# Router products on raw turned rows, softmax and the two largest in two parts, and an early indirect transfer

## The reference, cut to what matters

```python
x = x + graph_attention(ctx, layernorm(x), ...)          # layer 1: two GAT layers, 8 heads
x = x + expert_ffn(layernorm(x), w_router, w_gate, w_up, w_down)   # layer 2
# expert_ffn, for each of the 1024 tokens h = layernorm(x):
probs = softmax(h @ w_router)         # 8 experts
weights, experts = top_k(probs, 2)    # the two largest
# out = sum over the two experts of weight * scale * ((silu-gated gate) * up) @ down
x = x + similarity_attention(ctx, layernorm(x), Wq, Wk, gamma)     # layer 3
x = x + attention_and_experts(layernorm(x), ...)                   # layer 4
```

## Time and profile before

| | us |
|---|---|
| median of 3 runs | 1102.59 |
| lowest and highest | 1101.93, 1104.66 |
| the profiled execution | 1102.88 |
| its span | 1101.0 |
| TensorE busy in the span | 1006.5 (91%) |
| VectorE busy | 868.8 (79%) |
| ScalarE busy | 613.7 (56%) |
| GpSimd busy | 430.9 (39%) |

### The profile page before, as it was taken

One profiled execution on the slowest core, in us unless ns is written; L12 is line 12 of the kernel. 1 busy time (PEld: TensorE's weight loads), 2 busy tenths in 40 slices (PEclk: granted clock), 3 DMA queues, 4 the chain that ended last, 5 costly groups with the idle time before them and its releaser, 6 DMA issues.

```text
span 1101.0 us, 20158 instructions
## 1 busy us (share of the span) xinstructions
PE 1006.5 (91%) x5934; PEld 821.6 (75%) x5934; DVE 868.8 (79%) x2642; ACT 613.7 (56%) x1748; POOL 430.9 (39%) x372
## 2 busy tenths in 40 slices
PE   4788877999996489999999999999998999999997
PEld 2455545466663368999999999999887888888886
DVE  6999996577773889878777877777868888788877
ACT  4789983533232377777787777777952222222231
POOL 5798892633321233323332333222422232233231
PEclk9968887699998699999999999999999999999999
DMA  9700003011113111010101000000011111111111
GB/s 286 257 1 2 1 2 110 27 47 49 44 39 117 60 39 49 1 39 2 49 1 40 13 23 1 2 1 1 15 30 29 44 43 52 48 43 44 56 43 38
DMA packets 49459, 49.25 MB, mean 45 GB/s; under 512 B 4896, under 2 KB 42464, under 8 KB 49376
## 3 DMA queue, kind: packets, MB, share of 16 engines
q1 hardware_dynamic: 45888, 40.83, 11.8%
q0 software_dynamic: 2208, 6.03, 1.8%
q10 hardware_dynamic: 1280, 1.38, 0.5%
HBM read 43.11 MB, written 5.11 MB: 44 GB/s over the span
## 4 chain that ended last, share of the span: by engine, by line
PE 71%; DVE 12%; ACT 7%; POOL 5%; issue 4%; DMA 1%; SPq 0%; DVEq 0%; ACTq 0%; POOLq 0%
PE bank L57 13%; PE bank L58 13%; PE bank L59 13%; PE bank L957 6%; PE bank L978 4%; PE bank L852 4%; PE bank L860 4%; PE bank L879 4%; PE bank L967 3%; PE bank L979 2%; POOL rest L1418 2%; POOL alpha L1421 1%; DVE alpha L1626 1%; ACT alpha L1069 1%; ACT alpha L1054 1%
## 5 line engine op out<-in xcount | busy, mean ns | idle before, releaser
L1483 POOL TENSOR_TENSOR rot_s<-swap,rq 128x512 f32<-128x512 f32 x64 | 88.5, 1384 | 194.7 <-ACT swap L1261 194.6
L1137 ACT ACTIVATE silu<-bank 128x512 f32<-128x512 f32 x66 | 39.4, 598 | 173.6 <-PE bank L59 173.6
L2066 DVE TENSOR_TENSOR o_ring<-bank,o_ring 128x256 fp32r<-128x256 f32 x128 | 54.2, 424 | 80.2 <-ACT o_ring L1290 78.7
L1274 ACT ACTIVATE prob<-prob,pmin 128x128 f32<-128x128 f32 (+1 forms) x256 | 113.3, 447 | 5.4 <-DVE pmin L2047 5.4
L957 PE MATMUL bank<-kv,norm 128*128 128x128 f32 (+1 forms) x512 | 106.1, 330 | 6.1 <-DVE norm L2040 5.9
L1889 DVE SCALAR_TENSOR_TENSOR xs<-bank,wt,xs 128x256 f32<-128x256 f32 x264 | 109.0, 476 | 0.1
L1439 POOL TENSOR_TENSOR gate_r<-gate_w,gate_r 128x256 fp32r<-128x256 f32 x31 | 36.4, 1175 | 177.3 <-ACT gate_r L1130 177.3
L1290 ACT ACTIVATE o_ring<-bank 128x256 fp32r<-128x256 f32 x128 | 48.3, 378 | 76.4 <-PE bank L979 76.3
L57 PE MATMUL bank<-wo_r,o_ring 128*128 128x256 f32 x256 | 82.5, 322 | 0.0
L1867 DVE TENSOR_TENSOR hidf<-silu,bank 128x512 f32<-128x512 f32 x66 | 45.4, 688 | 44.9 <-ACT silu L1137 43.2
L2059 DVE TENSOR_SCALAR prob<-prob,pinv 128x128 f32<-128x128 f32 (+1 forms) x256 | 76.9, 343 | 4.6
(11 more groups left out here) (304 smaller groups left out, 3087.0 us busy)
## 6 DMA issues: line engine op xcount, KB each, us to landing
gate_w<-in_Wg SPq DMA_DIRECT2D x33, 128.0 KB, 2.1
up_w<-in_Wu SPq DMA_DIRECT2D x33, 128.0 KB, 2.3
down_w<-in_Wd SPq DMA_DIRECT2D x33, 128.0 KB, 2.3
w_all<-in_w_gate SPq DMA_DIRECT2D x8, 512.0 KB, 10.5
w_all<-in_w_up SPq DMA_DIRECT2D x8, 512.0 KB, 10.3
w_all<-in_w_down SPq DMA_DIRECT2D x8, 512.0 KB, 10.6
wq_g<-in_Wq SPq DMA_DIRECT2D x4, 1024.0 KB, 5.8
wo_g<-in_Wo SPq DMA_DIRECT2D x4, 1024.0 KB, 5.5
```

The lines of the kernel that those rows point to most:

```text
L1274: ins = act.activation(prob[:, u % 4, nt * P:nt * P + (nt + 1) * P], prob[:, u % 4, nt * P:nt * P + (nt + 1) * P], ACT.Exp, bias=pmin[:, u ...
L1483: pool.tensor_tensor(rot_s[:, m % 2].rearrange("p (b n) -> p b n", b=2), swap[:, m % 2].rearrange("p (b n) -> p b n", b=2), bcast(tab[:, 1 ...
```

## The change

There are four parts. First, `turn_graph` turns `xs` (raw rows) and not `norm`; the mean is taken out of the router's weights instead (`router_means` on TensorE and a subtraction on VectorE into `wr0`), and rstd is multiplied into the logits. Second, TURN_AT and ROUTE_AT of graphs 0 to 2 are other steps. Third, softmax and the two largest are done for the first six tiles (LEAD) and then for the last two, whose logits go to bank 3; `normalise_graph(B - 1)` goes behind the weights in `router0`, and five memsets go ahead of the last `add_x1`. Fourth, GpSimd sends one indirect transfer of a constant row to `xg` before its wait for the stores. SP's program is not changed.

```diff
-        NORM_AT, TURN_AT, ROUTE_AT = (ALL, ALL + 2, ALL + 10), (ALL + 2, ALL + 4, ALL + 11), (ALL + 4, ALL + 6, ALL + 12)
+        NORM_AT, TURN_AT, ROUTE_AT = (ALL, ALL + 2, ALL + 10), (ALL + 1, ALL + 3, ALL + 7), (ALL + 4, ALL + 6, ALL + 8)
+        LEAD = T - NT
                 def turn_graph(b):
-                    pe.wait_ge(S["norm_done"], NT * b + NT)
+                    pe.wait_ge(S["x1_added"], b + 1)
...
-                                              norm[:, NT * b + nt, c * P:c * P + P], ident[:])
+                                              xs[:, NT * b + nt, c * P:c * P + P], ident[:])
                     mm.then_inc(S["normT_ready"], NT)
+                def router_means():
+                    pe.wait_ge(S["const_in"], 16 * 5)
+                    pe.wait_ge(S["mean_set"], 1)
+                    pe.wait_ge(S["z_copied"], ALL)
+                    for c in range(HC):
+                        mm = pe.matmul(bank[2][:, T * E0:(T + 1) * E0], work[:, 0:P], wr0[:, c, :], start=c == 0, stop=c == HC - 1)
+                    mm.then_inc(S["wr_mean"], 1)
                 def route_graph(b):
                     pe.wait_ge(S["normT_copied"], NT * b + NT)
                     if b == 0:
-                        pe.wait_ge(S["const_in"], 16 * 5)
-                        pe.wait_ge(S["z_copied"], ALL)
+                        pe.wait_ge(S["wr_centred"], 1)
                     for t in range(NT * b, NT * b + NT):
+                        dst = bank[3][:, (t - LEAD) * E0:(t - LEAD + 1) * E0] if t >= LEAD else bank[2][:, t * E0:(t + 1) * E0]
...
+                    if b == B - 2:
+                        mm.then_inc(S["lead_ready"], 1)
...
+                    if k == ROUTE_AT[0] - 2:
+                        router_means()
 # ScalarE
+            act.wait_ge(S["lead_max"], 1)
+            act.activation(route[:, 0, 0:LEAD, 0:E0], route[:, 0, 0:LEAD, 0:E0], ACT.Exp).then_inc(S["lead_exp"], 1)
             act.wait_ge(S["rmax_done"], 1)
-            act.activation(route[:, 0, :, 0:E0], route[:, 0, :, 0:E0], ACT.Exp).then_inc(S["rexp_done"], 1)
+            act.activation(route[:, 0, LEAD:T, 0:E0], route[:, 0, LEAD:T, 0:E0], ACT.Exp).then_inc(S["rexp_done"], 1)
 # GpSimd
+            pool.memset(first_row[:], 0).then_inc(S["row_set"], 1)
+            pool.wait_ge(S["row_set"], 1)
+            pool.indirect_dma_start(
+                out=xg[:, 2, 0:P], out_offset=None, in_=ident_in,
+                in_offset=bass.IndirectOffsetOnAxis(ap=first_row[:], axis=0)).then_inc(S["xg_lead"], 16)
+            pool.wait_ge(S["xg_lead"], 16)
             pool.wait_ge(S["rows_out"], 16 * B)
 # VectorE, in the loop: normalise_graph(b) of graphs 0 to 2 goes ahead of elu(j)
+                    if k == ROUTE_AT[0] - 1:
+                        dve.wait_ge(S["wr_mean"], 1)
+                        dve.tensor_tensor(wr0[:], wr0[:], bcast(bank[2][:, T * E0:(T + 1) * E0], 1, HC), ALU.subtract
+                                          ).then_inc(S["wr_centred"], 1)
                     if (r := round_at(k, 20)) is not None:
+                        if r == 2 * B - 1:
+                            dve.wait_ge(S["g_elu"], QUADS * 2 * B)
+                            dve.memset(ones[:], 1.0)
+                            dve.memset(padded[:], -1.0)
+                            dve.memset(marks[:, :, T:], 0.0)
+                            chain.link(dve.memset(same_e[:], 1.0))
+                            dve.memset(same_e[:, :, 0:1], 0.0)
                         add_x1(r)
...
                 measure(2 * B - 1)
-                dve.memset(ones[:], 1.0)
...
-                normalise_graph(B - 1)
                 chain.restart()
+            def scaled_logits(ts, logits, ready, rms, done):
+                R = route[:, 0, ts, 0:E0]
+                dve.wait_ge(ready, 1)
+                dve.wait_ge(S["x_rms"], rms)
+                chain.link(dve.tensor_tensor(R, logits.rearrange("p (t e) -> p t e", e=E0), bcast(rstd[:, ts], 2, E0), ALU.mult))
+                chain.link(dve.tensor_reduce(rcol[:, 0, ts], R, X, ALU.max))
+                dve.tensor_tensor(R, R, bcast(rcol[:, 0, ts], 2, E0), ALU.subtract).then_inc(done, 1)
+            def two_largest(ts, ready):
+                R = route[:, 0, ts, 0:E0]
+                dve.wait_ge(ready, 1)
+                chain.link(dve.tensor_reduce(rcol[:, 1, ts], R, X, ALU.add))
+                chain.link(dve.reciprocal(rcol[:, 2, ts], rcol[:, 1, ts]))
+                chain.link(dve.tensor_tensor(padded[:, ts, 0:E0], R, bcast(rcol[:, 2, ts], 2, E0), ALU.mult))
+                for t in range(ts.start, ts.stop):
+                    dve.max(rtop[:, t, :], padded[:, t, 0:8])
...
+                for t in range(ts.start, ts.stop):
                     dve.match_replace(kept[:, t, :], rtop[:, t, :], padded[:, t, :], -2.0)
...
+                scaled_logits(slice(0, LEAD), bank[2][:, 0:LEAD * E0], S["lead_ready"], 2 * B - 1, S["lead_max"])
+                two_largest(slice(0, LEAD), S["lead_exp"])
+                scaled_logits(slice(LEAD, T), bank[3][:, 0:NT * E0], S["logit_ready"], 2 * B, S["rmax_done"])
+                two_largest(slice(LEAD, T), S["rexp_done"])
                 dve.tensor_tensor(chosen, kept[:, :, 0:E0], padded[:, :, 0:E0], ALU.not_equal).then_inc(S["chosen_done"], 1)
...
                 dve.scalar_tensor_tensor(weight, chosen, 0.25, padded[:, :, 0:E0], ALU.mult, ALU.mult)
+                normalise_graph(B - 1)
                 dve.wait_ge(S["count_ready"], 1)
 # VectorE, at the kernel's start
+            dve.memset(work[:, 0:P], 1.0 / D).then_inc(S["mean_set"], 1)
```

More of the change, by code:

```diff
@@ L127, in build @@
         eps = sb("eps", [P, 2])
+        first_row = sb("first_row", [P, 1], I32)
         minus_half = sb("minus_half", [P, NT])
@@ L1569, in finish_second, with normalise_graph @@
                 chain.link(dve.tensor_scalar(bT1[:], bT[:], -1.0, None, ALU.add))
+            def normalise_graph(b):
+                dve.wait_ge(S["x_rms"], B + b + 1)
+                for t in (NT * b, NT * b + 1):
+                    dve.tensor_scalar(norm[:, t, :], xs[:, t, :], mv[:, t, 0:1], rstd[:, t:t + 1],
+                                      ALU.subtract, ALU.mult).then_inc(S["norm_done"], 1)
             def graph_attention():
@@ L1667, in add_x1 @@
                     dve.tensor_tensor(rows, FEAT[:], rows, ALU.add).then_inc(S["x1_added"], 1)
[L1669 to L1674, removed]
                 measure(0)
@@ L1703, in graph_attention @@
                         divide(j)
+                    for b in range(B - 1):
+                        if k == NORM_AT[b]:
+                            normalise_graph(b)
                     if (j := quad_at(k, 4)) is not None:
                         elu(j)
+                    if k == ROUTE_AT[0] - 1:
+                        dve.wait_ge(S["wr_mean"], 1)
+                        dve.tensor_tensor(wr0[:], wr0[:], bcast(bank[2][:, T * E0:(T + 1) * E0], 1, HC), ALU.subtract
+                                          ).then_inc(S["wr_centred"], 1)
                     if (r := round_at(k, 20)) is not None:
+                        if r == 2 * B - 1:
[5 more added lines that the diff above has]
+                            dve.memset(same_e[:, :, 0:1], 0.0)
                         add_x1(r)
@@ L1720, in graph_attention @@
-                chain.restart()
-            def router0():
-                R = lambda j: route[:, j, :, 0:E0]
-                logits = bank[2][:, 0:T * E0].rearrange("p (t e) -> p t e", t=T)
-                dve.wait_ge(S["logit_ready"], 1)
-                chain.link(dve.tensor_reduce(rcol[:, 0, :], logits, X, ALU.max))
-                dve.tensor_tensor(R(0), logits, bcast(rcol[:, 0, :], 2, E0), ALU.subtract).then_inc(S["rmax_done"], 1)
-                dve.wait_ge(S["rexp_done"], 1)
-                chain.link(dve.tensor_reduce(rcol[:, 1, :], R(0), X, ALU.add))
-                chain.link(dve.reciprocal(rcol[:, 2, :], rcol[:, 1, :]))
-                chain.link(dve.tensor_tensor(padded[:, :, 0:E0], R(0), bcast(rcol[:, 2, :], 2, E0), ALU.mult))
-                for t in range(T):
+                chain.restart()
@@ L1737, in router0 @@
                 chain.link(dve.engine_nop())
-                chain.link(dve.memset(rtop[:, :, K0:8], -1.0))
-                for t in range(T):
+                chain.link(dve.memset(rtop[:, ts, K0:8], -1.0))
+                for t in range(ts.start, ts.stop):
                     dve.match_replace(kept[:, t, :], rtop[:, t, :], padded[:, t, :], -2.0)
                 chain.link(dve.engine_nop())
+            def router0():
+                scaled_logits(slice(0, LEAD), bank[2][:, 0:LEAD * E0], S["lead_ready"], 2 * B - 1, S["lead_max"])
+                two_largest(slice(0, LEAD), S["lead_exp"])
+                scaled_logits(slice(LEAD, T), bank[3][:, 0:NT * E0], S["logit_ready"], 2 * B, S["rmax_done"])
+                two_largest(slice(LEAD, T), S["rexp_done"])
```

11 lines of the change are left out of this document (2 added, 9 removed).

## The result

The changed kernel took 1106.93 us (median of 12 runs, 1106.16 to 1108.53) and the kernel before 1104.34 beside it; the ratio is 1.0031 (95% interval 1.0022 to 1.0039). By this ratio, which is not the quotient of the two medians, it is 3.4 us slower; the medians lie 2.6 us apart. The forecast was 6.2 us slower. Two further pairings of the same kernel, on two chips, gave 1.0061 (1.0048 to 1.0074) and 1.0051 (1.0038 to 1.0064). By the ratios the loss is 3.4, 6.7 and 5.6 us, by the medians 2.6, 6.2 and 5.6. The profiled execution took 1106.48 us for a span of 1104.3.

A forecast was written before the change was run, and what follows sets the result against it. The bound was taken as the chain to ScalarE's first gathered-row copy, then TensorE. The choice's -1.55 us drops off the path and the late loads add 6.2 us: 1108.8 us from a median of 1102.59, range 1105.2 to 1111.2.

The forecast's parts named there:

- Part 1: Last graph's raw rows are turned without waiting for statistics and normalise: 3.0 us gained on the way to the logits.
- Part 2: Earlier turn and route steps in the loop: last exponentials 1.5 us later, last sum 2.0 us late.
- The upper bound: 3.5 us for the late last sum, if TensorE falls to 1.2 GHz already during route(1).
- Part 3: Softmax and two largest in two parts on VectorE: choice 1.55 us earlier, whatever TensorE's clock.
- Part 4: Last normalise behind the weights: norm_done 7.5 us later, 10.12 us to first high part, gathered copy 6.2 us later.
- Part 5: GpSimd's early indirect transfer: worth nothing, at most 0.1 us, and delays no load.
- The sum: Choice 1.55 us earlier but no longer last, path 6.2 us longer: 1109.1 us profiled, 1108.8 on the median.
- three signs of being wrong: SP issues weights before 188, wk_g lands within 6 us of norm_done, or the mixture's products begin before 209.
- A: Weights not late enough to matter, shorter router counts: -1.55 us, 1101.0; needs wk_g by 192; chance 0.04.
- B: ScalarE's wait for the turned graph hidden, or load 2 to 3 us quicker: +4.1 to 4.2, 1106.7; chance 0.17.
- C: Split router's choice comes no earlier, norm_done at 192.4: +7.8, 1110.4, or 1111.0 at old tile spacing; chance 0.15.
- D: Short load: wk_g lands 4.3 us behind its issue, not 7.9: +2.6, 1105.2; chance 0.08.

The follow-up runs named there:

- after_again: The changed kernel with nothing altered, profiled and paired with the kernel before a second time: 1109.96 us, ratio 1.0061.
- before_loads_first: The kernel before with SP issuing the weights at x1_added, ahead of the store of graph 3, rq and rk: 1104.28 us, ratio 1.0005.
- norm_early: The changed kernel with the last normalise straight behind the leading six tiles' logits, not behind the weights; SP unaltered: 1105.18 us, ratio 1.0014.
- before_late_loads: The kernel before with SP's store of graph 3 and the five loads behind it also waiting for earlier_done: 1108.97 us, ratio 1.0058.
- loads_first: The changed kernel with SP issuing wq_g, wk_g and wv_g ahead of the store of graph 3, rq and rk: 1101.83 us, ratio 0.9982.
- one_part: turns_late with softmax and the two largest in one part over all eight tiles: 1100.51 us, ratio 0.9979.
- turns_late: loads_first with later turn and route steps, so copies of turned graphs stand behind the exponentials on ScalarE: 1100.41 us, ratio 0.9978.
- turns_no_indirect: turns_late without GpSimd's early indirect transfer, its memset and both waits: 1100.93 us, ratio 0.9975.
- turns_late_only: The changed kernel with only the steps of turns_late, loads left late: 1107.33 us, ratio 1.0034.

## Why the prediction was right, and where its size was off

The sign and the mechanism were right, and the time lies in the range. Step by step:

- Part 1, the gain on the way to the last logits. From the last sum's end to the transposes it takes 0.04 us in the chain of after. Right.
- Part 2, the last sum 2.0 us later: the copy, the exponentials behind it and the late last sum are all there. Against before it was 1.5 us at full clock (after_again, last exponential +1.5 as worked out) and 2.8 to 2.9 where TensorE weighed group 14 at 1.2 GHz; against before_loads_first, at 1.2 GHz too, it was 2.0 to 2.1 us. The upper bound took the clock as a risk from 178 us on; the place where it mattered was the weighing at 167.6, ahead of the wait, and this the prediction did not name.
- Part 3, the choice 1.55 us earlier: 0.9, 2.3 and 0.9 us in the three profiles. It said that TensorE's clock does not matter for it. From the last sum on no profile of the changed kernel tests this: the last turn (1.11 to 1.12 us) and the last logits (1.87 to 1.88) were made at half clock in all three, and the choice came 7.48 to 7.49 us behind the last sum's start. For it speaks that even at half clock the last logits were made by 185.0 us in the chain of after and VectorE took them up at 185.76, busy until then. The last sum itself does hang on the clock.
- Part 4, norm_done 7.5 us later: 8.1, 6.7 and 8.1. Right, and the normalise itself is hidden: 0.24 us of VectorE's wait for the counts are left where 0.77 were the earlier trace rows.
- Part 4, from norm_done to the first high part 10.12 us, as before: the term that was mis-sized. It took 8.8, 9.0 and 9.1 us. The trace of before had one sample of it, and it was on the slow side; wk_g landed in 6.9 to 7.2 us and not 7.9. This is 1.0 to 1.3 us of the error. The five transfers hold 1920 KB, which is 1.97 MB and not 1.8. The Trainium skill, "DMA: Bandwidth & Descriptors", section "Anatomy of one DMA", gives its figure for one DMA issued from GpSimd; put to SP's five together it made the prediction's estimate of 6.3 us, 6.5 with 1.97 MB. The traces do not agree: 8.1 us is the least of the eight profiles with this order of SP.
- Part 4, from there to the gathered copy: 12.61 us in the earlier trace rows, 11.3 predicted, 11.13 measured in all three. The similarity tiles come 0.72 us apart when TensorE is ahead, so their spacing before was TensorE's. The prediction did not name what lies behind this: before, the copy hung on the choice, and the loads had 1.5 us to spare.
- Part 5: worth nothing. Right for this kernel. It said that the transfer delays no load; that holds for the time at which it is sent, and not in norm_early.
- The sum: in the first profile norm_done is 8.05 us later, the distance to the first high part 1.31 shorter and that to the copy 1.48 shorter, which makes +5.3. With the two others it is +5.3, +4.1 and +5.6 us from the last edge minimum, against 6.2, and 4.1 to 4.8 at equal clock. By the ratios 3.4, 6.7 and 5.6. That the median of 1106.93 lies as near as 1.9 us to the forecast of 1108.8 is in part luck: the forecast was counted from 1102.59, the median of 3 runs, and beside the change the kernel before took 1104.34; counted from that it would have been 1110.5. None of the three signs of being wrong appeared: SP issued the weights from 190.9 us, the first high part came 8.8 us behind norm_done, and the first expert product at 209.94, where 212.8 was forecast.
- Rivals. A (the loads don't matter) needed wk_g within 1.2 us of norm_done; before_late_loads and loads_first rule it out. B is the closest in time: it said 1106.7 and +4.1 to 4.2, and after_again's copy is at +4.1. Neither of its conditions held as given: ScalarE's wait was there (2.90 us), and the loads were quicker by 1.0 to 1.3 us and not 2 to 3. So the first median fell near B by other terms than B's. C (the choice comes no earlier) does not hold: it came 0.9 to 2.3 us earlier, though the split itself gives only 0.46 us by one_part. D (a short load) does not hold at 8.1 us or more.

## What to carry to other kernels

Before an instruction is moved into a gap where its engine waits anyway, list who waits for its semaphore, and what stands behind that wait on every queue: here a normalise of 0.74 us was nearly free on VectorE and cost about 6 us through the loads issued behind it (the copy at +40.9, and at +34.8 with the loads moved). Work out also what these loads had to spare: here 1.5 us. When a step and the loads behind it share a queue for no reason but the order of lines, move the loads. Two faults on one chain show as one loss: the change that lost 0.3 to 0.6% gains 0.18% with the loads moved (loads_first) and 0.22 to 0.25% with the copies behind the exponentials as well (turns_late and turns_no_indirect, 1100.4 and 1100.9 us, against 1103.8 for before). The medians can't tell the last two figures from the first; the second fault is shown by the profiles, and by turns_late_only, whose runs (1104.8 to 1108.2 us) hardly overlap those of the changed kernel beside it (1107.9 to 1109.3).

## What the runs showed of the hardware that I had not expected

An indirect transfer of 0.07 MB, in which all 128 partitions fetch the same row of DRAM, landed in 3.7 to 3.9 us alone and in 6.6 us beside loads in norm_early, and these loads took 10.4 us where they took 8.1 without it. It depends on when it is sent: in turns_late it went out 1.1 us behind the last of three loads and landed in 4.7 us, and wk_g landed in 5.4 us against 5.2 in turns_no_indirect. The gathers of rows from `x_rows` in before, with twice its bytes each, landed in 2.7 to 3.0 us. That the partitions share one source row was not varied by itself, so its part is open.

The same products in the same kernel ran at 1.2 GHz in one execution and at 2.4 in another (1.93 and 1.07 us for 16), 1.27 us on the path in the one place where ScalarE waited for them. The graph rounds ahead of the last edge minimum differed by up to 4.8 us between profiles; a single profile's absolute times would have given the change 3.4 us where the distance within the stage gave 5.3.
